# Two chained attention and feed-forward layers: operands loaded by chunk, position rows made once, four small moves between engines

## The chip, the cores and the metric

The kernel runs on one core of a Trainium2 chip. The metric is the device time in microseconds (us) of one execution; lower is better. The core has a matmul engine (TensorE, PE), VectorE (DVE), ScalarE (ACT), GpSimd (POOL) and SyncE (SP), which issues DMAs here; each runs its own list of instructions in order and waits on semaphores for the others.

## The reference

All matrices have 256 columns, x has 2048 rows. Cut to what matters:

```python
xn = layernorm(x)
s  = linear_attention(xn)              # cumulative sums over the rows, 16 heads of 16
g  = silu(xn @ ternary(weight).T + b)
x  = x + s * g                         # layer 0
xn = layernorm(x)
q, k, v = split(xn @ qkv_w.T + qkv_b)  # 16 heads of 16 columns
scores = q @ k.T / 4 + slope[h] * (pos_k - pos_q), causal
s  = softmax(scores) @ v @ out_w.T + out_b
# 8 experts, the top 2 of each row:
y_e = (glu * sigmoid(1.702 * glu) * (lin + 1)) @ w2[e].T + b2[e]
g  = silu(sum over the two chosen e of weight_e * y_e)
x  = x + s * g                         # layer 1
```

## The kernel before

**Layer 0** runs over four chunks of 512 rows (`NC` = 4, `CH` = 512). In each engine's list `front(c)` has the projections and cumulative sums of a chunk and `back(c)` the quotient, the gate and the sum into x. On ACT the order is `front(c + 1)`, `high_parts(c)` (first halves of two experts' first weights), `back(c)` (L685 to L694). On DVE it is `front(c + 1)`, `back(c)`, `gate(c)` (L985 to L995), and `gate(c)` reads what ACT's `back(c)` writes. On POOL it is `front(c + 1)`, `low_parts(c)` (second halves of those weights, which count up `w1l_done`), `back(c)`. SP issues 23 DMAs at L339 that fill the buffer of routed rows `x_rows` with zeros, and then, in a loop over chunks, waits for `w1l_done`, fetches the next two experts' raw weights (L326) and stores x (L351).

**Projection of layer 1** (L712 to L731, L1027 to L1041, L1327 to L1348) makes q and k of a chunk as three bf16 parts each, in `QP`, which is part of the operand tile `OPS`. SP stores them in the DRAM tensor `parts` (L357). When all four chunks are stored, `load(h)` (L360) reads the operands of a head back into `OPS` with six DMAs, three for each side; each takes one, two or three parts, or one part several times over (`LOADS`, L35), 48, 32 or 16 partitions of 4 KB. Four head slots exist, so `load` runs for two heads (a pair) at a time, and the next pair but one is loaded when the scores of a pair are done (L423 to L427). Twelve more operand rows carry position times slope: ACT makes them for heads 0 to 3 (`first_of`, L763), POOL for the others (`rows`, L524).

**Main loop** (`for n in range(STEPS)` in the lists of all engines, 684 steps). A pair of heads has 80 tiles (`PER_PAIR`), there are 8 pairs, 640 tiles. Step n has

- `score_a(n)` on PE and `reduce_a(n)` on DVE: scores of 128 rows against up to 512 keys, only for the row maxima. The tile lies in one of four banks for n < 44 (`WIDE`), then in one of two, so `score_a(n)` waits for `reduce_a(n - 2)` (L1422).
- `score_b(n - 44)` on PE and `exponential(n - 44)` on ACT (`LEAD` = 44): the same scores transposed, less the row maxima, in two banks; `values` multiplies them with v, four tiles at a time.
- At the end of a chunk of A tiles: `row_maxima` (DVE), `maxima` (POOL, L536), `turn_maxima` (PE, at the steps `TURN_AT`), `max_rows` (ACT) and `rows_out` (SP, two DMAs at L377), which puts the maxima into the operands that B tiles of this chunk use 44 steps later. `ORDER` is the order of a pair's chunks; chunk a has 8 (a + 1) tiles.
- Every 20 steps one block of 256 routed rows: `fetch_block` on SP (five DMAs, L403 to L407), `up` and `down` on PE, `gate_tanh`, `gate_linear`, `expert_out` on ACT, `glu`, `linear` on DVE, `store_block` on SP. There are 23 blocks; block b starts at step 84 + 20 b, is fetched at step 66 + 20 b or earlier, as SP's list allows. `down` and `turn_maxima` and the heads' outputs share bank 7.

Between projection and main loop the routing is worked out: ranks of the logits and one-hot rows (DVE, L1079 to L1110), first parts of x (ACT, L773) and second parts (POOL, L560), 32 indirect DMAs that scatter the rows (POOL, `scatter`, L565), and the experts' output biases, by weights turned on PE, matmuls and copies on ACT (L776 to L784). In the last pair POOL gathers the experts' results (`gather`, L573), two indirect DMAs for each of 16 row tiles, 12 of them before `maxima(28)` (L600), and DVE sums them (`add_experts`, L1065). The end of the kernel projects and gates the output.

Of the kernel before, what the change touches and what calls it, by code (L numbers as in the profile page):

```python
# [14 lines left out]
ALU = mybir.AluOpType  # L15
# [3 lines left out]
P = 128  # L19
# [17 lines left out]
ROWS_B = ROWS_A + 3  # L37

ORDER = (0, 3, 1, 2)
# [12 lines left out]
FIRST_BLOCK, EVERY = 84, 20  # L52
# [30 lines left out]
TURN_AT = {chunk_end(m) - 1 + (3, 4, 5, 3)[m % NC]: m for m in range(NC * PAIRS)}  # L83
HEADS_AT = {chunk_end(m) - 1 + LEAD + (15, 11, 11, 11)[m % NC]: m for m in range(NC * PAIRS)}
BLOCK_AT = {FIRST_BLOCK + EVERY * b: b for b in range(BLOCKS)}
DOWN_AT = {n + 14: b for n, b in BLOCK_AT.items()}
FETCH_AT = {n - 18: b for n, b in BLOCK_AT.items()}
STORE_AT = {n + 1: b for n, b in DOWN_AT.items()}
STEPS = TOTAL + LEAD
END_PAIRS = [2 * c + r for c in ORDER for r in range(2)]  # L90
END_AT = {650: 0, 655: 1, 661: 2, 665: 3, 675: 4, 679: 5}
ADD_AT = {FIRST_BLOCK + EVERY * BLOCKS + 28 + 3 * n: t
          for n, t in enumerate([2 * q + r for q in END_PAIRS for r in range(2)])}
GATHERS = 6
# [8 lines left out]
def build(nc, x, w_qkv0, w_out0, w_ffn, b_ffn, w_qkv1, b_qk1, b_v1, w_out1, b_out1, slopes, pos_rows, pick,  # L103
          masks, ident, sel, table, gate_w, gate_b, w1, b1, w2, b2, out):
    ctx = ExitStack()
    with ctx:
# [3 lines left out]
        def sem(name):  # L110
# [39 lines left out]
        TH = sb("TH", [P, 2, CH])  # L150
        GT = sb("GT", [P, 2, CH])
# [9 lines left out]
        WE = sb("WE", [P, NT, E])  # L161
# [22 lines left out]
        XTH, XTL = XT[:, 0], XT[:, 1]  # L184
        WQG = 3 * D + E
# [9 lines left out]
        WET = pr32[:, 0:S]  # L195
        B2 = pr32[:, S:S + D]
        TAB = pr32[:, S + D:S + D + E * NT + 8 + 24]
# [7 lines left out]
        YB = xt32[:, 0:1024].rearrange("p (b n) -> p b n", b=2)  # L205
        GB = xt32[:, 1024:1024 + 512 * GATHERS].rearrange("p (g a d) -> p g a d", g=GATHERS, a=2)
# [18 lines left out]
        QV = ops32[:, 0:2048].rearrange("p (m n) -> p m n", m=4)  # L225
        QR = ops32[:, 2048:4096].rearrange("p (m n) -> p m n", m=4)
        QP = ops32[:, 4096:7168].bitcast(BF16).rearrange("p (m j n) -> p m j n", m=4, j=3)


        parts = nc.dram_tensor("qk_parts", (2, 3, D, S), BF16, kind="Internal").ap()  # L230
        x_rows = nc.dram_tensor("x_rows", (SLOTS * BLOCKS, 2 * D), F16, kind="Internal").ap()
# [29 lines left out]
        v_copied, lg_copied, gsplit, route = (  # L261
            sem("v_copied"), sem("lg_copied"), sem("gsplit"), sem("route"))
        expd, rstep, ones_rows, we_done, wet_ps = (
            sem("expd"), sem("rstep"), sem("ones_rows"), sem("we_done"), sem("wet_ps"))
        wet_copied, b2_ps, acc_init, b1_prep, slope_part = (
            sem("wet_copied"), sem("b2_ps"), sem("acc_init"), sem("b1_prep"), sem("slope_part"))
        scl, opa_rows, vs_ready, a_scored, a_reduced = (
            sem("scl"), sem("opa_rows"), sem("vs_ready"), sem("a_scored"), sem("a_reduced"))
# [8 lines left out]
        hot, count_ps, chain, slots_done, xr_high, xr_low = (  # L277
            sem("hot"), sem("count_ps"), sem("chain"), sem("slots_done"), sem("xr_high"), sem("xr_low"))
# [10 lines left out]
        b2_zero, wet_zero = sem("b2_zero"), sem("wet_zero")  # L289
# [3 lines left out]
        ones_in, first_rows = sem("ones_in"), sem("first_rows")  # L293
# [27 lines left out]
        def _(sp):  # L321
# [1302 lines left out]
```

## Time and profile before

| | us |
|---|---|
| median of 3 runs (970.33 to 974.29) | 972.36 |
| profiled execution, its own time | 969.48 |
| its span | 967.7 |

Busy time over the span and idle time before the costliest groups, of the page of the profile:

```profile
span 967.7 us, 13783 instructions
...
PE 796.4 (82%) x4910; PEld 387.1 (40%) x4910; DVE 635.3 (66%) x1197; ACT 498.7 (52%) x1030; POOL 313.9 (32%) x363
...
PE   4474659914889999999999999999999995888986
PEld 1242345403324444444544444444444432222543
DVE  5999997665856666676566667666666763984121
ACT  2343315861555565555555655555565552556340
POOL 2766963121660060051006005100600516340111
PEclk9797979966799999999999999999999997999795
DMA  9501302332223235225223532522353112111110
```

Each digit is the busy share of one of 40 slices of 24.2 us, in tenths; PEclk is the clock granted to TensorE, DMA the mean share of the 16 DMA engines. The first eight slices are layer 0 and the projection, slices 9 and 10 are a hole in PE's row, then comes the main loop, with PE at nine tenths, and the last six slices are the last pair of heads and the output.

### The profile page before, as it was taken

Reading aid. Unit: us, or ns where it says so; the run is one execution under the profiler, and the core shown is the slowest. Engines: PE = TensorE matmul, PEld = TensorE weight load, DVE = VectorE, ACT = ScalarE, POOL = GpSimd, SP = SyncE. Lnnn points to the kernel's source line nnn. Section 1 sums busy time; section 2 is a strip of 40 time slices with the busy share of each in tenths; the row PEclk is TensorE's granted clock in tenths of the full one; section 3 lists DMA queues with packets and bytes.
Section 4 is the critical chain, followed back from the end, with each engine's and each line's share of the span. In section 5 each row is a group of like instructions: output and inputs, shape, how many; then the busy total and the mean of one; then the engine's idle time right before and its main releaser. Section 6 shows DMA issues by size and latency. Waiting matters only on the chain.

```text
span 967.7 us, 13783 instructions
## 1 busy us (share of the span) xinstructions
PE 796.4 (82%) x4910; PEld 387.1 (40%) x4910; DVE 635.3 (66%) x1197; ACT 498.7 (52%) x1030; POOL 313.9 (32%) x363
## 2 busy tenths in 40 slices
PE   4474659914889999999999999999999995888986
PEld 1242345403324444444544444444444432222543
DVE  5999997665856666676566667666666763984121
ACT  2343315861555565555555655555565552556340
POOL 2766963121660060051006005100600516340111
PEclk9797979966799999999999999999999997999795
DMA  9501302332223235225223532522353112111110
GB/s 322 173 0 66 109 22 87 131 108 70 102 93 88 67 99 100 76 63 107 62 66 103 101 73 65 106 62 66 98 108 71 40 49 77 45 55 68 42 34 33
DMA packets 72392, 80.03 MB, mean 83 GB/s; under 512 B 33561, under 2 KB 56020, under 8 KB 72196
## 3 DMA queue, kind: packets, MB, share of 16 engines
q1 hardware_dynamic: 67660, 68.84, 26.0%
q0 software_dynamic: 3296, 8.62, 2.9%
q10 hardware_dynamic: 1368, 1.70, 0.6%
q8 instruction: 39, 0.64, 0.3%
q14 instruction: 29, 0.24, 0.1%
HBM read 34.22 MB, written 26.74 MB: 63 GB/s over the span
## 4 chain that ended last, share of the span: by engine, by line
PE 55%; DVE 26%; issue 7%; POOL 3%; DMA 3%; ACT 3%; SPq 1%; POOLq 0%; ACTq 0%; DVEq 0%
PE bank L1466 14%; DVE PM L1163 11%; PE bank L1424 10%; PE bank L1444 7%; PE bank L1361 5%; PE bank L1371 5%; PE bank L1481 3%; DVE PR L960 3%; PE bank L1256 2%; PE bank L1508 2%; DMA OPS<-qk_parts 2%; DVE YT L1062 2%; POOL XT L580 1%; POOL x_rows L569 1%; PE bank L1427 1%
## 5 line engine op out<-in xcount | busy, mean ns | idle before, releaser
L1163 DVE TENSOR_REDUCE PM<-bank 128x1 f32<-128x512 f32 (+3 forms) x640 | 368.6, 605 | 217.7 <-PE bank L1427 160.1
L811 ACT ACTIVATE PR<-bank 128x512 f32<-128x512 f32 (+3 forms) x640 | 331.6, 536 | 302.7 <-PE bank L1447 150.7
L1424 PE MATMUL bank<-OPS 108*128 108x512 bf16 (+3 forms) x640 | 228.5, 361 | 72.3 <-DVE PM L1163 36.1
L1444 PE MATMUL bank<-OPS 111*128 111x512 bf16 (+3 forms) x640 | 225.0, 354 | 3.3 <-ACT PR L811 3.1
L1466 PE MATMUL bank<-PR,VS 128*17 128x512 f32 (+3 forms) x1280 | 159.0, 548 | 0.5 <-ACT PR L811 0.4
L540 POOL TENSOR_TENSOR NP<-NM,NIL 128x8 bf16<-128x8 f32 x32 | 6.5, 202 | 429.9 <-DVE NM L1171 429.8
L1424 PEld LDWEIGHTS bank<-OPS 108*128 108x128 bf16 x640 | 64.2, 100 | 193.3 <-DVE PM L1163 131.9
L1361 PE MATMUL bank<-WB 128*128 128x256 f16 x552 | 90.7, 272 | 0.0
L527 POOL TENSOR_TENSOR OPS<-POSR,SCL 12x2048 bf16<-12x2048 bf16 x24 | 87.8, 3680 | 7.6 <-PE bank L1447 7.6
L1444 PEld LDWEIGHTS bank<-OPS 111*128 111x128 bf16 x640 | 63.3, 99 | 39.0 <-ACT PR L811 15.6
L1361 PEld LDWEIGHTS bank<-WB 128*128 128x128 f16 x552 | 49.5, 99 | 44.6 <-issue 22.3
L1427 PE MATMUL bank<-MASK 128*128 128x128 bf16 x256 | 57.7, 225 | 0.0
L1447 PE MATMUL bank<-MASK 128*128 128x128 bf16 x256 | 57.4, 225 | 0.0
L1299 PE MATMUL bank<-VV,YT 128*128 128x256 f32 x64 | 21.4, 506 | 36.1 <-DVE YT L964 36.1
L1256 PE MATMUL bank<-XT,VV 128*128 128x512 f16 x144 | 35.2, 407 | 13.1 <-issue 11.6
L1371 PE MATMUL bank<-WB,YT 128*128 128x256 f32 x184 | 45.9, 392 | 0.0
L1481 PEld LDWEIGHTS bank<-SEL,U 128*128 128x128 f32 x256 | 32.1, 197 | 26.3 <-issue 26.3
L1371 PEld LDWEIGHTS bank<-WB,YT 128*128 128x128 f32 x184 | 33.1, 189 | 23.1 <-issue 19.5
L1466 PEld LDWEIGHTS bank<-PR,VS 128*17 128x17 f32 x1280 | 21.3, 96 | 49.2 <-issue 29.0
L580 POOL DMA_INDIRECT XT<-y_rows,SLOT x32 | 30.9, 966 | 18.2 <-DVE ACC L1075 9.8
L1481 PE MATMUL bank<-SEL,U 128*128 128x34 f32 x256 | 35.7, 286 | 0.8 <-ACT U L800 0.8
L569 POOL DMA_INDIRECT x_rows<-XT,SLOT x32 | 31.0, 968 | 14.1 <-issue 9.1
(187 smaller groups left out, 975.8 us busy)
## 6 DMA issues: line engine op xcount, KB each, us to landing
qk_parts<-OPS SPq DMA_DIRECT2D x16, 384.0 KB, 3.6
OPS<-qk_parts SPq DMA_DIRECT2D x32, 192.0 KB
x_rows<-PR SPq DMA_DIRECT2D x23, 256.0 KB, 3.6
WB<-W1H SPq DMA_DIRECT2D x23, 256.0 KB, 2.4
WB<-W1L SPq DMA_DIRECT2D x23, 256.0 KB, 2.4
WB<-in_w SPq DMA_DIRECT2D x23, 256.0 KB, 2.7
y_rows<-XT SPq DMA_DIRECT2D x23, 256.0 KB, 2.2
OPS<-qk_parts SPq DMA_DIRECT2D x32, 128.0 KB
```

The source lines that it names most:

```text
L527: pool.tensor_tensor(OPS[0:POS, h % 4, side, :], POSR[:, side, :], SCL[:, side, h:h + 1].broadcast_to([POS, S]), ALU.mult).then_inc(opa_ro ...
L811: act.activation(PR[:, tile % RING, off:CH], PS[2 + tile % 2][:, off:CH], ACT.Exp).then_inc(b_exped, 1)
L1163: dve.tensor_reduce(PM[:, c % 2, j, xq, gg:gg + 1], bank[:, 0:width], AX.X, ALU.max).then_inc(a_reduced, 1)
L1256: done = mm(out, w if weight_first else d, d if weight_first else w, start=first and k == 0 and j == 0, stop=last and k == KK - 1 and j == 2)
L1361: last = mm(PS[5 + f][:, SLOTS * part:SLOTS * part + SLOTS], W1B[b % 2][:, wp, col:col + P], XB[b % 2][:, dp, k, :], start=j == 0, stop=j ...
L1371: last = mm(PS[7][:, D * q:D * q + D], YT[:, b % 2, f, P * q:P * q + P], W2B[b % 2][:, f, :], start=f == 0, stop=f == KK - 1)
L1424: last = mm(bank[:, 0:width], OPS[0:ROWS_A, h % 4, 0, P * (TC * a + xq):P * (TC * a + xq) + P], OPS[0:ROWS_A, h % 4, 1, CH * gg:CH * gg + ...
L1427: last = mm(bank[:, P * xq:P * xq + P], MASK[:, 0, :], MASK[:, 2, :], start=False, stop=True)
L1444: last = mm(bank[:, off:CH], OPS[0:ROWS_B, h % 4, 1, P * k:P * k + P], OPS[0:ROWS_B, h % 4, 0, CH * b + off:CH * b + CH], start=True, stop ...
L1447: last = mm(bank[:, off:off + P], MASK[:, 1, :], MASK[:, 2, :], start=False, stop=True)
L1466: last = mm(PS[4][32 * n:32 * n + HD + 1, off:CH], VS[:, (2 * p + j) % 4, k, :], PR[:, (first + n) % RING, off:CH], start=b > 0 and k0 == ...
L1481: last = mm(PS[7][:, wide * q:wide * q + wide], U[:, m % 2, P * q:P * q + P], SEL[:, :], start=True, stop=True)
```

## The change

- `load(h)` stays for heads 2 and up. Heads 0 and 1 are loaded by chunk of 512 rows (`first_load(c)`, 14 DMAs each), issued by SP between the stores of the parts. For that `QV`, `QR`, `QP` move out of `OPS`. `score_a` waits for the chunk alone that it needs.
- The position rows of all heads are made once: POSR has 96 partitions (8 heads of 12), ACT makes four tiles of 96x2048 in layer 0 (`position_rows`), SP stores them in DRAM, and each `load` has a seventh DMA that reads them. The slopes' parts (`prepare`, DVE) move into layer 0.
- The 23 DMAs of zeros move behind the first wait for `w1l_done` on SP.
- `rows_out` moves from SP to ACT, one step after `max_rows`.
- The output bias of an expert is fetched with its block (`B2B`) and added by DVE as it empties the block's bank (`expert_out` moves from ACT to DVE); the turned weights, their matmuls and copies go.
- A tiles use three banks from tile 44 on; both halves of a block's first product use one bank, the second half nine steps behind the first. `fetch_block` waits for `ye_copied`, the copy of the block two before, instead of `ye_ps`, and has six DMAs.
- `ORDER` becomes (0, 1, 2, 3); blocks start at step 88 + 20 b, are fetched at 72 + 20 b; scatters and gathers are dealt out otherwise between the `maxima`.
- Ranks are worked out by chunk (5 operations each), the rest of the sort is 28 small operations, two in a step of the main loop.

```diff
             sp.dma_start(TAB[:, :], table).then_inc(table_in, 16)
-            sp.wait_ge(memset_done, 11)
-            for r in range(0, SLOTS * BLOCKS // P, 2):
-                sp.dma_start(x_rows[P * r:P * r + 2 * P, :].rearrange("(r p) c -> p r c", p=P),
-                             NAUGHT[:, :].unsqueeze(1).broadcast_to([P, 2, 2 * D])).then_inc(rows_zero, 16)
-
             for c in range(NC):
                 if c + 2 < E // 2:
                     sp.wait_ge(w1l_done, 2 * c + 2)
                     fetch_experts(c + 1)
+                if c == 0:
+                    sp.wait_ge(memset_done, 11)
+                    for r in range(0, SLOTS * BLOCKS // P, 2):
+                        sp.dma_start(x_rows[P * r:P * r + 2 * P, :].rearrange("(r p) c -> p r c", p=P),
+                                     NAUGHT[:, :].unsqueeze(1).broadcast_to([P, 2, 2 * D])).then_inc(rows_zero, 16)
+                    for n in range(4):
+                        sp.wait_ge(rows_made, n + 1)
+                        sp.dma_start(all_rows[n // 2, :, n % 2, :], PROWS[n % 2]).then_inc(rows_kept[n % 2], 16)
...
+            def first_load(c):
+
+                cols = slice(CH * c, CH * c + CH)
+                sp.wait_ge(parts_out[0], 16 * c + 16)
+                sp.wait_ge(parts_out[2], 16 * c + 16)
+                for h in range(2):
+                    sp.dma_start(OPS[0:POS, h, :, cols], all_rows[0, POS * h:POS * h + POS, :, cols]).then_inc(first_in[c], 16)
+                    for side in range(2):
...
+            for c in range(NC):
+                cols = slice(CH * c, CH * c + CH)
+                for m in range(4):
...
+                    sp.wait_ge(qk_p2, 4 * c + m + 1)
+                    sp.dma_start(parts[side, :, half * P:half * P + P, cols].rearrange("j f t -> f j t"),
+                                 QP[m]).then_inc(parts_out[m], 16)
+                if c:
+                    first_load(c - 1)
+            first_load(NC - 1)
...
                 if b >= 2:
-                    sp.wait_ge(ye_ps, b - 1)
+                    sp.wait_ge(ye_copied, b - 1)
...
             for n in range(STEPS):
-                if n - 1 in TURN_AT:
-                    rows_out(TURN_AT[n - 1])
                 if n in FETCH_AT:
                     fetch_block(FETCH_AT[n])
...
-            scatter(range(0, 5))
+            scatter(range(0, 4))
             maxima(1)
-            scatter(range(5, 11))
+            scatter(range(4, 12))
             maxima(2)
-            scatter(range(11, NT))
+            scatter(range(12, NT))
             maxima(3)
...
-                    gather(0, GATHERS)
+                    gather(0, 3)
                 maxima(NC * p)
                 if p == PAIRS - 1:
-                    gather(GATHERS, 11)
+                    gather(3, 8)
...
+            def position_rows():
+
+                act.wait_ge(scl, 6)
+                act.wait_ge(cast_in, 32)
+                for n in range(4):
+                    if n >= 2:
+                        act.wait_ge(rows_kept[n % 2], 16)
+                    act.activation(PROWS[n % 2], POSR[:, n % 2, :], ACT.Copy, scale=SCL[:, n % 2, n // 2:n // 2 + 1])\
+                        .then_inc(rows_made, 1)
...
                 high_parts(c)
+                if c == 0:
+                    position_rows()
                 back(c)
...
                 if tile < WIDE:
                     wait(pe, a_reduced, tile - 3)
                 else:
-                    pe.wait_ge(a_reduced, tile - 1)
-                bank = PS[tile % 4] if tile < WIDE else PS[tile % 2]
+                    pe.wait_ge(a_reduced, tile - 2)
+                if tile == WIDE:
+                    pe.wait_ge(sorting, SORTED)
+                bank = PS[tile % 4] if tile < WIDE else PS[(0, 1, 6)[tile % 3]]
```

## Rows read from the trace of the kernel before

**Rows 1.** Busy time by stretch: from:to, length, engines, TensorE's clock, DMA share, GB/s
```profile
198.00:230.00 32.00, 0.08 (x2) 0.06 (x2) 15.11 (x46) 12.47 (x17) 10.51 (x12) 0.54 0.33 110
...
313.60:398.10 84.50, 78.96 (x552) 38.91 (x550) 55.37 (x108) 49.29 (x108) 19.25 (x26) 1.00 0.35 82
...
796.30:884.00 87.70, 69.20 (x419) 23.92 (x416) 60.55 (x124) 42.60 (x88) 35.33 (x52) 0.88 0.17 49
```
**Rows 2.** Waits of PE from 313.6 to 778 us: total, times, longest
```profile
PE bank L1424 <- DVE PM L1163: 24.8, 56, 1.0
```
**Rows 3.** Timeline, layer 0: start, length, engine, line, operation
```profile
54.89 0.59 ACT L671 ACTIVATE TH<-bank 128x512 f32<-128x512 f32 x1
...
60.54 2.36 DVE L970 SCALAR_TENSOR_TENSOR GT<-TH,GT 128x512 f32<-128x512 f32 x2
...
60.80 1.55 POOL L476 TENSOR_TENSOR PR<-OPS 128x512 f32<-128x512 f32 x1 [7.30 <-DVE YT L964]
...
73.36 2.14 POOL L505 TENSOR_TENSOR W1L<-W1L,W1H 128x1024 f16<-128x1024 f32 x1
...
75.52 0.36 SPq L326 DMA_DIRECT2D W1H<-in_w  x1
```
**Rows 4.** Timeline, SP's zeros, and busy time while they are moved
```profile
15.27 18.43 SPq L339 DMA_DIRECT2D x_rows<-PR  x23
...
20.00:32.00 12.00, 7.38 (x40) 3.74 (x37) 11.72 (x36) 6.19 (x13) 7.99 (x6) 1.00 1.08 379
```
**Rows 5.** Groups by form, ACT, 198 to 260 us: count, then busy, mean ns
```profile
L766 ACT ACTIVATE OPS<-POSR,SCL 12x2048 bf16<-12x2048 bf16 x8 | 15.3, 1987 | 4.7 <-DMA qk_parts<-OPS 4.7
```
**Rows 6.** Timeline, DVE: part of `prepare`; one form alone, then beside POOL
```profile
160.67 0.77 DVE L1020 SCALAR_TENSOR_TENSOR SCL<-SLP,PICK,SCL 12x16 f32<-12x16 bf16 x4
...
207.26 0.28 DVE L1097 TENSOR_TENSOR U<-U,LG 128x128 f32<-128x128 f32 x1
...
217.15 1.19 DVE L1107 TENSOR_TENSOR U<-U,TOP 128x128 f32<-128x128 f32 x1
```
**Rows 7.** Timeline and busy time, loads of heads 0 to 3 and PE's first score
```profile
203.20 12.05 SPq L369 DMA_DIRECT2D OPS<-qk_parts  x12
...
229.97 0.27 PE L1424 MATMUL bank<-OPS 108*128 108x128 bf16 x1 [31.92 <-DMA OPS<-qk_parts]
...
203.00:230.00 27.00, 0.03 (x1) 0.06 (x2) 10.65 (x28) 11.94 (x13) 10.51 (x12) 0.50 0.22 72
```
**Rows 8.** First pair: the line of the B scores; timeline of reductions, scatters, step 80
```profile
L1444 PE MATMUL bank<-OPS x640: 219/379/634, 259.0 to 941.5; 111*128 111x512 bf16 x128, 111*128 111x256 bf16 x32
...
244.36 12.30 DVE L1163 TENSOR_REDUCE PM<-bank 128x1 f32<-128x512 f32 x22
...
244.41 0.99 POOL L569 DMA_INDIRECT x_rows<-XT,SLOT  x1 [0.30 <-issue]
...
293.08 0.22 PE L1424 MATMUL bank<-OPS 108*128 108x128 bf16 x1
```
**Rows 9.** Timeline, SP in the main loop, then one landing of L407
```profile
430.98 11.99 SPq L369 DMA_DIRECT2D OPS<-qk_parts  x12
...
452.28 5.43 SPq L407 DMA_TRANSPOSE WB<-x_rows  x1
...
DMA to landing us min/median/max: 9.3/9.3/9.3
```
**Rows 10.** Timeline, last pair: gathers and PE's wait, and clock behind it
```profile
799.07 1.04 POOL L580 DMA_INDIRECT XT<-y_rows,SLOT  x1 [0.56 <-issue]
...
815.47 0.27 PE L1474 MATMUL bank<-MASK,NP 128*24 128x128 bf16 x1 [10.23 <-POOL NP L548]
...
815.50:822.00 6.50, 6.50 (x27) 2.62 (x27) 3.06 (x6) 2.43 (x5) 1.93 (x2) 0.52 0.13 33
```
**Rows 11.** Prices: issue on SP; DVE from a bank, by form
```profile
L377 SPq DMA_DIRECT2D OPS<-MT x64: 698/762/2429, 255.8 to 888.7; - x64
...
L978 DVE SCALAR_TENSOR_TENSOR GT<-bank,GT 128x512 f32<-128x512 f32 x8 | 5.3, 680 | 0.6 <-PE bank L1299 0.6
```

More of the change, by code:

```diff
@@ L351, in _ @@
                 sp.dma_start(x1_dram[:, TC * c:TC * c + TC, :], XO[:, TC * c:TC * c + TC, :]).then_inc(x1_spill, 16)
-            with sp.Fori(0, NC) as c:
-                for m in range(4):
-                    side, half = m // 2, m % 2
-                    sp.wait_ge(qk_p2, 4 * c + m + 1)
-                    sp.dma_start(parts[side, :, half * P:half * P + P, ds(c * CH, CH)].rearrange("j f t -> f j t"),
-                                 QP[:, m, :, :]).then_inc(parts_out[m], 16)
             def load(h):
+                sp.dma_start(OPS[0:POS, h % 4, :, :], all_rows[h // 8, POS * (h % 8):POS * (h % 8) + POS, :, :]).then_inc(
+                    opa_in[h // 2 % 2], 16)
                 for side in range(2):
@@ L387, in _ @@
                              ONEB[0:3, :].unsqueeze(1).broadcast_to([3, NC, CH])).then_inc(ones_in, 16)
+            for m in range(4):
+                sp.wait_ge(parts_out[m], 16 * NC)
             load(2)
@@ L517, in _ @@
             rstd(2 * NC, ds(TC * (NC - 1), TC))
-            pool.wait_ge(outT, 2 * NC)
-            pool.memset(WET[:, :], 0.0).then_inc(wet_zero, 1)
-            scale(E // 2 - 1)
-            pool.wait_ge(w1l_done, E - 2)
-            low_parts(E // 2 - 1)
-            def rows(h):
-                for side in range(2):
-                    pool.tensor_tensor(OPS[0:POS, h % 4, side, :], POSR[:, side, :],
-                                       SCL[:, side, h:h + 1].broadcast_to([POS, S]), ALU.mult).then_inc(opa_rows, 1)
             def head_values(h):
@@ L1021, in prepare @@
                                                  ALU.mult, ALU.add).then_inc(scl, 1)
[L1023 to L1025 removed]
+            front(0, True)
+            for c in range(NC):
+                if c + 1 < NC:
+                    front(c + 1, c + 2 < NC)
+                if c == NC - 1:
+                    gated(c - 1)
+                    norm_apply(0, NC)
+                back(c)
+                gate(c)
+                if c:
+                    next_stats(c - 1)
@@ new lines, in rank @@
+            def rank(c, k):
+                tiles = slice(TC * c, TC * c + TC)
+                own = LG[:, tiles, :].unsqueeze(3).broadcast_to([P, TC, E, E])
+                other = LG[:, tiles, :].unsqueeze(2).broadcast_to([P, TC, E, E])
+                lower = TAB[:, E * NT + 32:].rearrange("p (e f) -> p e f", e=E).unsqueeze(1).broadcast_to([P, TC, E, E])
+                if c == 0 and k == 0:
+                    dve.wait_ge(table_in, 16)
+                if k == 0:
+                    dve.wait_ge(lg_copied, TC * c + TC)
+                wait(dve, ranked, 5 * c + k)
+                if k == 0:
+                    ins = dve.tensor_tensor(RIVAL, other, own, ALU.is_gt)
+                elif k == 1:
+                    ins = dve.tensor_tensor(EQUAL, other, own, ALU.is_equal)
+                elif k == 2:
+                    ins = dve.tensor_tensor(EQUAL, EQUAL, lower, ALU.mult)
+                elif k == 3:
+                    ins = dve.tensor_tensor(RIVAL, RIVAL, EQUAL, ALU.add)
+                else:
+                    ins = dve.tensor_reduce(RANK[:, tiles, :], RIVAL, AX.X, ALU.add)
+                ins.then_inc(ranked, 1)
@@ L1069, in add_experts @@
                 dve.wait_ge(y_gathered[place % GATHERS], 32 * (place // GATHERS + 1))
-                if place == 0:
-                    dve.wait_ge(acc_init, NT // 2)
-                for a in range(2):
-                    if a:
-                        dve.wait_ge(half_added, place + 1)
-                    dve.scalar_tensor_tensor(
-                        ACC[:, t, :], GB[:, place % GATHERS, a, :], WTS[:, a, t:t + 1],
-                        ACC[:, t, :], ALU.mult, ALU.add).then_inc(y_added if a else half_added, 1)
@@ L1157, in reduce_a @@
+                ins.then_inc(sorting, 1)
             def reduce_a(tile):
```

436 lines of the change are left out of this document (198 added, 238 removed).

## The prediction

> **What bounds the kernel now.** I read the busy times by stretch first. There is a hole: from 198 to 230 us TensorE is all but idle, and a pair of the main loop takes 84.50 us with TensorE busy 78.96 [rows 1]. So the main loop is TensorE's, the hole is somebody else's. The timeline names it: the first score ends a wait of 31.92 us for the operands [rows 7]. Next the waits of PE in the loop: 24.8 us in 5.5 pairs, 4.5 us a pair, for reductions of DVE [rows 2]; there is no other wait of size. Last the lists of ACT, POOL and SP wherever the change moves something, since a moved DMA takes its place in a queue with it. In layer 0 DVE works without a break, so a microsecond lost there is lost at the end.
>
> Times below are against the profiled execution: 969.48, of which 967.7 is the span; the median of the runs, 972.36, is 2.9 above it, and I add that at the end.
>
> **1. Layer 0: position rows and zeros.** ACT's new `position_rows` stands between `high_parts(0)` and `back(0)`. Its third tile reuses the first one's buffer and waits until SP's store of the first has landed. On SP that store now stands behind the wait for `w1l_done` of 2, the fetch of two experts and the 23 zeros. Before, `w1l_done` reached 2 at 75.5 (73.36 + 2.14), and SP's fetch starts then [rows 3]. ACT's `back(0)` began at 54.89 and DVE's gate, which needs it, at 60.54 [rows 3]. So the wait that is added queues ACT's gate of chunk 0 behind it, and DVE behind that. In order:
> - DVE first runs `prepare`, 11 operations, four of which took 0.77 [rows 6]: 2.1 us. It then releases POOL at 62.9 instead of 60.8; with DVE idle POOL's six products and two differences run undisturbed. I take 74.7 for `w1l_done` (bounds 73 and 77.6).
> - The experts are 1 MB, 2.8 us at the 379 GB/s of the zeros' stretch [rows 4], say 3.5 with their start: 79 us. The zeros took 18.43 us to issue, paced by the queue, 6.0 MB at that rate being 15.9 us [rows 4]: I take 16.5, so 95.5. The store behind them needs some 2.5 us to land: 98. Then two tiles of 1.92 us (15.3 for 8) [rows 5]: 102. ACT's tanh and copy give the first gate 1.1 later, 103.
> - DVE starts its gate at 103 instead of 60.5: 42.5 us. It gets some back, since POOL has finished what disturbed it: a form that takes 0.28 alone took 1.19 beside POOL [rows 6]. I take 4.5 off.
>
> Sum: **+38** (bounds 33 and 44). The earlier place of the zeros hid them beside DVE's work; the new one has no cover, as ACT, DVE and PE all wait for it. The larger POSR load (eight times the rows) is among the first DMAs, which fill the engines: +1.
>
> **2. The hole.** Operands of chunk 0 are issued after the stores of chunk 1, near 176, 14 DMAs; 12 took 12.05 us [rows 7], 1 us each, though the first came faster, so 10 to 14 us a chunk against chunks that come every 11 to 12 us. `first_load(0)` lands before 190; the score of tile 0 can start when projection ends, at 198.5, 31.5 us earlier. The later chunks (needed at tiles 8, 24 and 48) keep ahead. What is late next is DVE: from 198.5 it must do two rankings (10 operations), 28 operations of sorting, and the first 44 reductions. 22 reductions took 12.30 us, 0.56 each [rows 8]: 24.6; 38 operations at 0.3, 11.4; and POOL's second parts of x now run beside them, +3. So tile 44 comes at 198.5 + 39 = 237.5, where the first B score was at 259.0 [rows 8]: 21.5 us are left. Next POOL: a scatter is issued every 1.26 us (0.99 and a pause of 0.30) [rows 8]. The second group is now 16 scatters, 20.2 us, after `maxima(1)` near 229; `maxima(2)` follows at 251 while PE wants it at step 52, near 243.5. A wait of 7, where there were two of 1.2 and 2.6 before: 4 us back. Step 80, at 293.1 before [rows 8], comes at 276: **-17** (bounds -8 and -25).
>
> **3. The main loop's waits.** With the third bank `score_a(n)` waits for the reduction of n - 3, one step (1.05 us) more slack than the longest wait of 1.0 [rows 2] needs: -4.5 a pair. DVE's new work, four bank emptyings a pair at 0.68 [rows 11], brings it from 55.4 to 58.1 of 82 us [rows 1]; it hides. ACT loses four copies and gains eight DMA issues a pair at 0.76 on SP [rows 11], two in a row 1.5 us; its B tiles have two banks, so about 1 us of slack: +0 to +1 each time, and +0.5 for `expert_out` ahead of a turn. A DMA issue on ACT between B tiles does not occur before; I take the price of SP's. Net -2.2 a pair, 6 pairs: **-13** (bounds -26 and +12).
>
> **4. Block fetches behind operand loads.** This is the edit I weigh most after the first. A pair's load is 2 heads of 768 KB. In the hole it ran at 72 GB/s with the DMA engines 0.22 busy [rows 7]: its copies of 48 and 32 partitions keep few engines busy, and what comes after on SP's queue waits for those. In the loop: load issued at 430.98, the block fetch that follows it has its last DMA issued at 452.28 and landed 9.3 later, 461.6: 30.6 us after the load began [rows 9]. Before, that fetch was for the block of step 84, 38 steps after the load's place at step 46, and nothing waited. Now count modulo 80: the load goes out when step 44 begins, as SP is free; a fetch stands at step 52 behind it and its block starts at step 68. 24 steps of 1.03 us are 24.7, plus 0.7 in the step. The fetch is whole at 31.4 (30.6 and the seventh DMA of each head): TensorE waits 6. It loses clock too: after the 10.23 us wait the clock was at 0.52, half of 2.4 GHz, for 6.5 us [rows 10]; for a wait of 6 I take 1.5 us. Five loads (pairs 1 to 5) have such a fetch, the sixth has none: 5 x 7.5 = **+38** (bounds 0, if the fetch overtakes the load, and +55).
>
> By the Trainium skill (DMA: Bandwidth & Descriptors, "Why a DMA increments its semaphore by 16 and not by 1") a copy runs on the largest number of engines up to 16 that divides both outer sizes, and on the lowest-numbered ones; that gives 3, 2 and 16 engines for the three shapes, so engine 0 carries a third, a half and a sixteenth of them. At that page's 27 GiB/s an engine (Specifications) the load would be an estimated 18 us, the fetch would be whole before step 68, and part 4 would be near 0. The row of 27 us says otherwise.
>
> **5. The last pair.** 12 gathers stood before `maxima(28)`, from 799.07, and TensorE waited 10.23 us [rows 10]. Now there are 6, 7.6 us after step 559, over before the turn at step 572. The wait goes, and with it half the 6.5 us at half clock; the third bank gives another 1: **-14** (bounds -5 and -20). Late next is DVE, 60.6 busy of 87.7 [rows 1]. GATHERS of 5 leaves 15 steps from gather to sum: enough.
>
> The rest (order of chunks, one bank for a block's halves, biases) I cost at +1, for the stores that queue behind `first_load`. A pair's 80 tiles are the same in any order.
>
> **Sum:** +38 +1 -17 -13 +38 -14 +1 = +34: 1003.5 for the profiled execution, 1006 for the median.
>
> **Rivals.**
> - A: block fetches don't wait. For it: block weights are copies on all engines, a small part on the busy ones. Against it: the 30.6 us of [rows 9]. 1006 - 38 = 968. The Trainium skill's figures, weighed in part 4, would give this case too.
> - B: layer 0 hides the position rows. It would need SP's store to land before 60 us, which the wait for `w1l_done` at 75.5 forbids [rows 3], or the zeros not to hold it up. The latter alone leaves 22 of 38. 1006 - 38 = 968, or with A as well 930.
> - C, on the slow side: ACT's DMA issues. Each of some 28 row maxima sent in the loop keeps ACT for 2 x 0.76 [rows 11]. Once ACT lags by more than the step that two B banks allow, all of that delay is TensorE's: 1.4 us each instead of the 0.5 counted above, 28 x 0.9 = 25 more, 1031.
> - D: the change does what it says and its gains stand alone, 930 to 940; that is A and B together.
>
> **How the numbers follow.** My forecast 0.64, A 0.17, B 0.07, A with B 0.04, C 0.08. Range 962 to 1032: it takes in A and B at 968, and the bounds of parts 1 and 4 above; their own range in the likeliest case is 985 to 1030. About 0.5% (5 us) is what a measurement here can tell from no change. Faster by more (below 967.5): half of A and B and all of A with B, 0.16. Within: the other half, 0.10. Slower: 0.74.
>
> **What would show it.** Part 1: ACT idle from about 59 to 98 us, its `back(0)` near 101, DVE idle over the same time and SP's 23 zeros starting near 76. Part 2: the first score at 198.5 plus the delay of part 1, PE waiting for `maxima(2)`. Part 3: no wait of `score_a` for DVE in the loop, small waits of `score_b` for ACT. Part 4: five waits of `up` for `block_in`, 6 us each, 80 steps apart, each with a fall of the clock. Part 5: no wait of 10 us at `maxima(28)`. I am wrong if DVE's gate of chunk 0 starts before 80 us, or if `up` never waits.

## The result and the profile after

The changed kernel takes 992.51 us in the median of 4 runs (990.12 to 996.16), the kernel before 971.35 beside it (969.40 to 974.29): a ratio of 1.0219, 95% interval 1.0176 to 1.0261. It is slower by 21 us. The profiled execution took 991.7, its span is 989.8. The forecast was 1006, with 962 to 1032 as range and 0.74 on slower.

The page of the changed kernel; each digit is a slice of 24.7 us:

```profile
span 989.8 us, 13708 instructions
...
PE   4520775795679997997899799969988999889996
DVE  6940799888857674675466466646664666797121
ACT  2330621584046653664455366535644555556541
PEclk9765887897579998999899899979998999999995
DMA  8009111144333046227223623362263231250000
```

Slices 3 and 4 of DVE (4, 0) and PE (2, 0) are a new hole in layer 0, where DVE stood at 9 before; the old hole, a 1 and a 4 in PE's slices 9 and 10, is now a 5 and a 6 in slices 10 and 11; and in the main loop PE drops to 8, 7 or 6 every few slices, and PEclk to 8 or 7 with it, where it had an unbroken row of nines. To see what each was worth I read the same milestones in every trace: the starts of `score_a` of tiles 0, 80 and 560 and of the last one, and the end. Here they are for the two kernels and the experiments on chips alike ("pairs" is tile 80 to tile 560, six pairs; "end" tile 560 to the end):

| kernel | median us | ratio, 95% | tile 0 | tile 80 | pairs | end |
|---|---|---|---|---|---|---|
| before | 971.35 | 1 | 230.0 | 293.1 | 503.1 | 171.5 |
| changed | 992.51 | 1.0219, 1.0176 to 1.0261 | 233.0 | 309.9 | 531.3 | 148.6 |
| e4_whole | 1022.26 | 1.0557, 1.0502 to 1.0611 | 265.4 | 336.5 | 529.9 | 152.7 |
| e5_two_banks | 1009.54 | 1.0407, 1.0351 to 1.0463 | 233.4 | 311.4 | 545.3 | 153.2 |
| e6_rows_sp | 1008.88 | 1.0402, 1.0348 to 1.0457 | 233.0 | 321.4 | 534.7 | 150.0 |
| e12_rows_again | 962.40 | 0.9915, 0.9891 to 0.9939 | 201.4 | 278.4 | 531.1 | 148.7 |
| e9_both | 916.77 | 0.9443, 0.9409 to 0.9476 | 205.0 | 280.9 | 481.4 | 152.6 |
| e10_both_two_banks | 943.57 | 0.9728, 0.9681 to 0.9775 | 204.1 | 281.2 | 508.4 | 151.3 |
| e11_both_rows_sp | 909.46 | 0.9374, 0.9328 to 0.9420 | 204.8 | 282.2 | 475.3 | 150.3 |
| e8_before_spread | 957.72 | 0.9880, 0.9829 to 0.9931 | 216.1 | 282.8 | 504.8 | 167.1 |

By it the change cost 16.8 up to tile 80, cost 28.2 in the six pairs, and gave 22.9 back at the end: 22.1 of span in all.

**Layer 0**, the timeline of the changed kernel: start, length, engine, line, in brackets the wait before it and who ended it. The first two lines are ACT's `position_rows`, then ACT's gate, DVE's gate, and SP's list.

```profile
55.49 3.88 ACT L683 ACTIVATE WB<-POSR,SCL 96x2048 bf16<-96x2048 bf16 x2
97.94 3.89 ACT L683 ACTIVATE WB<-POSR,SCL 96x2048 bf16<-96x2048 bf16 x2 [38.56 <-DMA position_rows<-WB]
101.74 0.57 ACT L673 ACTIVATE TG<-bank 128x512 f32<-128x512 f32 x1
...
102.83 0.69 DVE L966 SCALAR_TENSOR_TENSOR TG<-TG 128x512 f32<-128x512 f32 x1 [41.03 <-ACT TG L674]
...
74.46 0.35 SPq L332 DMA_DIRECT2D W1H<-in_w  x1
74.85 0.43 SPq L332 DMA_DIRECT2D W1L<-in_w  x1
75.32 18.04 SPq L350 DMA_DIRECT2D x_rows<-PR  x23
93.41 8.75 SPq L354 DMA_DIRECT2D position_rows<-WB  x4
...
148.39 37.87 SPq L360 DMA_DIRECT2D x_rows<-XO  x3
```

Read from below: SP could not store a position row before its fetch at 74.46 and the zeros, 18.04 long. The first store goes out at 93.41 and ACT goes on at 97.94; so ACT stood 38.56 and DVE 41.03. The last store of x ends at 186.26 (148.39 + 37.87); in the kernel before it ended at 150.71:

```profile
112.91 37.80 SPq L351 DMA_DIRECT2D x_rows<-XO  x3
```

**The main loop**, waits of PE in it (total, times, longest), and the first of the long ones with the fetch that ended it; L1381 is `up`, L1423 `score_a`, L1443 `score_b`:

```profile
PE bank L1381 <- DMA WB<-x_rows: 38.5, 5, 9.3
PE bank L1443 <- ACT PR L806: 7.0, 6, 1.2
PE bank L1423 <- DVE PM L1181: 1.8, 5, 0.4
...
351.65 0.37 SPq L364 DMA_DIRECT2D OPS<-position_rows  x1
...
371.16 6.88 SPq L431 DMA_TRANSPOSE WB<-x_rows  x1
...
DMA to landing us min/median/max: 3.4/7.2/11.1
...
382.28 0.82 PE L1381 MATMUL bank<-WB 128*128 128x256 f16 x3 [6.49 <-DMA WB<-x_rows]
```

The load goes out at 351.65, the last DMA of the fetch behind it at 371.16 and lands 11.1 later (the largest of the two in that window), at 382.3: 30.6 us after the load began, as in [rows 9]. PE's waits for DVE that stood in [rows 2] are gone but for 1.8 us.

### The profile page after: what moved, and what is told of

Same layout as the page of the kernel before. It is cut to its first block, busy times and chain, and to the rows that moved or that the text cites. A ratio compares the mean times of both kernels' runs of the same rounds, so it can differ in the third digit from the quotient of the medians.

```text
span 989.8 us, 13708 instructions
## 1 busy us (share of the span) xinstructions
PE 793.1 (80%) x4861; PEld 379.6 (38%) x4862; DVE 623.2 (63%) x1208; ACT 474.6 (48%) x991; POOL 227.9 (23%) x337
## 4 chain that ended last, share of the span: by engine, by line
PE 45%; DVE 15%; SPq 11%; POOL 8%; DMA 8%; issue 8%; ACT 4%; ACTq 1%; POOLq 0%; DVEq 0%
PE bank L1465 10%; PE bank L1443 9%; PE bank L1423 7%; SPq L373 6%; DMA WB<-x_rows 6%; PE bank L1381 5%; PE bank L1391 4%; POOL XT L587 3%; DVE PR L956 3%; POOL x_rows L576 2%; PE bank L1480 2%; SPq L350 2%; PE bank L1322 2%; PE bank L1506 2%; ACT PR L806 2%
## 5 line engine op out<-in xcount | busy, mean ns | idle before, releaser
L1181 DVE TENSOR_REDUCE PM<-bank 128x1 f32<-128x512 f32 (+3 forms) x640 | 364.4, 604 | 228.2 <-PE bank L1426 127.8
L806 ACT ACTIVATE PR<-bank 128x512 f32<-128x512 f32 (+3 forms) x640 | 327.3, 534 | 324.6 <-PE bank L1443 203.2
L1423 PE MATMUL bank<-OPS 108*128 108x512 bf16 (+3 forms) x640 | 234.1, 371 | 16.3 <-DVE PM L1181 15.2
L1443 PE MATMUL bank<-OPS 111*128 111x512 bf16 (+3 forms) x640 | 227.4, 358 | 13.1 <-ACT PR L806 11.1
L1381 PE MATMUL bank<-WB 128*128 128x256 f16 x552 | 94.1, 280 | 38.5 <-DMA WB<-x_rows 38.5
L1423 PEld LDWEIGHTS bank<-OPS 108*128 108x128 bf16 x640 | 66.1, 103 | 111.1 <-DVE PM L1181 87.0
L1443 PEld LDWEIGHTS bank<-OPS 111*128 111x128 bf16 x640 | 63.2, 99 | 89.0 <-ACT PR L806 65.9
L1381 PEld LDWEIGHTS bank<-WB 128*128 128x128 f16 x552 | 49.4, 100 | 77.3 <-DMA WB<-x_rows 40.7
L1279 PE MATMUL bank<-XT,VV 128*128 128x512 f16 x144 | 37.3, 425 | 12.9 <-DVE XT L868 12.4
L1322 PEld LDWEIGHTS bank<-VV,YT 128*128 128x128 f32 x64 | 17.1, 275 | 74.9 <-ACT TG L674 52.6
L1480 PEld LDWEIGHTS bank<-SEL,U 128*128 128x128 f32 x256 | 31.0, 191 | 26.2 <-issue 21.7
L966 DVE SCALAR_TENSOR_TENSOR TG<-TG 128x512 f32<-128x512 f32 x8 | 7.4, 954 | 41.3 <-ACT TG L674 41.3
```

What stands on the lines that cost most here:

```text
L806: act.activation(PR[:, tile % RING, off:CH], PS[2 + tile % 2][:, off:CH], ACT.Exp).then_inc(b_exped, 1)
L1181: dve.tensor_reduce(PM[:, c % 2, j, xq, gg:gg + 1], bank[:, 0:width], AX.X, ALU.max).then_inc(a_reduced, 1)
L1322: last = mm(PS[6 + r][:, D * q:D * q + D], OT0[:, k, P * (2 * r + q):P * (2 * r + q) + P], WO0[:, k, :], start=k == 0, stop=k == KK - 1)
L1381: last = mm(PS[5][:, SLOTS * part:SLOTS * part + SLOTS], W1B[b % 2][:, wp, col:col + P], XB[b % 2][:, dp, k, :], start=j == 0, stop=j == 5)
L1423: last = mm(bank[:, 0:width], OPS[0:ROWS_A, h % 4, 0, P * (TC * a + xq):P * (TC * a + xq) + P], OPS[0:ROWS_A, h % 4, 1, CH * gg:CH * gg + ...
L1443: last = mm(bank[:, off:CH], OPS[0:ROWS_B, h % 4, 1, P * k:P * k + P], OPS[0:ROWS_B, h % 4, 0, CH * b + off:CH * b + CH], start=True, stop ...
```

## The experiments

Four kernels (e1, e2, e3, e7) fell on a chip on which every kernel is longer: the kernel before took 992.43 there (987.07 to 996.03), against 970 to 971 elsewhere. The traces say in part how. Waits of PE in e3_spread, 200 to 340 us:

```profile
PE bank L1441 <- issue: 6.9, 3, 2.9
PE bank L1441 <- ACT PR L804: 6.8, 3, 3.3
PE bank L1421 <- issue: 4.0, 8, 1.6
```

"issue" means that the engine waited for nothing the profile shows. In e9_both, elsewhere, the same code and stretch has 0.6 us of it. These pauses sit in the first pair and the last, hardly in the loop. Times there scatter more too, and the traces of e1 and e7 are of their shortest executions (990.45 and 1002.15). So of these four I read ratios to the kernel before on the same chip, and from the traces layer 0 and the loop.

**One part of the wait in layer 0.** The zeros go back to their old place, the stores of position rows stay behind the wait for `w1l_done`.

```diff
             sp.dma_start(TAB[:, :], table).then_inc(table_in, 16)
+            sp.wait_ge(memset_done, 11)
+            for r in range(0, SLOTS * BLOCKS // P, 2):
+                sp.dma_start(x_rows[P * r:P * r + 2 * P, :].rearrange("(r p) c -> p r c", p=P),
...
             for c in range(NC):
...
                 if c == 0:
-                    sp.wait_ge(memset_done, 11)
-                    for r in range(0, SLOTS * BLOCKS // P, 2):
...
```

> The changed kernel with the 23 DMAs of zeros back in their old place, ahead of the wait for w1l_done; the four stores of the position rows stay behind that wait. It splits the wait: theory says the stores start at 75 us instead of 93.4 and land near 80, so 17 to 18 us of ACT's 38.6 us wait go and 20 stay; 974 to 977 us. If the zeros were no part of it, nothing changes and it is 992; if they were all of it, 957.

Measured: 1000.16, ratio 1.0089 (1.0052 to 1.0127); against 1.0219 that is 1.3%, 12.6 us, where 15 to 18 were expected. In the trace the last store of x ends at 170.51, 15.75 earlier than in the changed kernel, and tile 0 starts at 217.0, 16.0 earlier:

```profile
131.26 39.25 SPq L360 DMA_DIRECT2D x_rows<-XO  x3
```

So the zeros are 16 us of the wait, and the rest is the wait for `w1l_done`.

**The whole of it.** The stores ahead of both.

```diff
             sp.dma_start(TAB[:, :], table).then_inc(table_in, 16)
+            for n in range(4):
+                sp.wait_ge(rows_made, n + 1)
+                sp.dma_start(all_rows[n // 2, :, n % 2, :], PROWS[n % 2]).then_inc(rows_kept[n % 2], 16)
             for c in range(NC):
...
-                    for n in range(4):
-                        sp.wait_ge(rows_made, n + 1)
...
```

> The changed kernel with one block of SP's list moved: the four stores of the position rows stand ahead of the wait for w1l_done, the fetch of two experts and the 23 zeros; all else as in the changed kernel. Theory (the order of SP's list makes the 41.0 us wait of DVE for ACT's first gate): the first store lands near 62 us, ACT's back(0) starts near 67 instead of 101.7, DVE waits some 5 us instead of 41, and the kernel is 30 to 36 us faster than the changed one, 957 to 962. Rival (the loss in layer 0 comes from the four tiles of 96x2048 and the larger load themselves): ACT is still late by more than 20 us and the kernel gains under 15.

> The changed kernel with the four stores of position rows ahead of the wait for w1l_done, once more, on another chip, since all engines of the chip of the first look stood still for 1 to 3 us at many places that no wait explains. From the kernel with both remedies (step 80 at 280.9 against 309.9) and the ratio of the first look (986.3 to 992.4) the edit is worth 27 to 30: 962 to 966.

Measured: 986.26 on the first chip, with four runs from 974.66 to 994.27, too far apart for a ratio; on another chip 962.40, ratio 0.9915 (0.9891 to 0.9939). Against the changed kernel's 992.5 that is 30 us, as expected, and tile 80 comes 31.5 earlier. Timeline of SP and DVE in e12:

```profile
62.09 2.19 SPq L345 DMA_DIRECT2D position_rows<-WB  x2
76.18 18.29 SPq L353 DMA_DIRECT2D x_rows<-PR  x23
117.12 37.80 SPq L360 DMA_DIRECT2D x_rows<-XO  x3
...
64.95 3.35 DVE L966 SCALAR_TENSOR_TENSOR TG<-TG 128x512 f32<-128x512 f32 x2 [3.22 <-ACT TG L674]
```

DVE's gate starts at 64.95 instead of 102.83, and of the 35.5 us that the last store of x had lost, 31.3 are back. With this one reordering the change is 0.9% faster than the kernel before.

**The block fetch behind the load.** The load's copies of 48 and 32 partitions become copies of 16.

```diff
                     for first, parts_of, times_of in LOADS[side]:
-                        src = parts[side, first:first + parts_of, HD * h:HD * h + HD, :]
-                        if times_of > 1:
-                            src = src.broadcast_to([times_of, HD, S])
-                        sp.dma_start(OPS[row:row + rows, h % 4, side, :], src).then_inc(opa_in[h // 2 % 2], 16)
+                        for part in list(range(first, first + parts_of)) * times_of:
+                            sp.dma_start(OPS[row:row + HD, h % 4, side, :],
+                                         parts[side, part, HD * h:HD * h + HD, :]).then_inc(opa_in[h // 2 % 2], 16)
+                            row += HD
```

> The changed kernel with each operand load for heads 2 and up cut into copies of 16 partitions (twelve for a head instead of six, the same bytes; first_load as it was). Theory (the copies of 48 and 32 partitions run on 3 and 2 DMA engines, so a pair's 1.5 MB take 27 us): the copies of 16 partitions run on 16 engines, the load takes as long as its 26 issues, 16 to 18 us, the DMA share while it runs rises, the fetch behind it is whole near step 65 of 68, and the waits of up for block weights fall from 38.5 to under 8 us: 957 to 968 us. Rival (the load is bound by its bytes or by DRAM): waits and time stay.

Measured: 971.33, ratio 0.9810 (0.9748 to 0.9872), 4.1% or 40 us below the changed kernel, where 25 to 35 were expected. The six pairs take 481.4 instead of 531.3, 49.9 less, and no wait of `up` for a DMA is left. Both remedies together:

> The changed kernel with two mends at once: the position rows' stores ahead of the wait on SP, and operand loads of heads 2 and up in copies of 16 partitions. If the two losses of the changed kernel are these and are independent, the gains add: 30 to 36 and 25 to 34 us, 925 to 937 us, some 4% under the kernel before the change.

Measured: 916.77, ratio 0.9443 (0.9409 to 0.9476); six pairs again 481.4, tile 80 29.0 earlier than in the changed kernel. Both kernels are beaten, by 5.6% the one before, and the 925 to 937 expected too. Against e12, which lacks the spread alone, the spread is worth 45.6 us; by the traces 49.7 in the six pairs, less 2.5 up to tile 80 and 3.9 behind tile 560, and no run resolves why those two are longer. What the edit did to the load is seen in the busy times of stretches: in the changed kernel load issued, fetch issued, fetch landing, in e9 load issued, then fetch issued and landed (the last two columns are the DMA share and GB/s).

```profile
351.60:363.90 12.30, 11.97 (x92) 6.83 (x90) 8.81 (x18) 6.38 (x16) 1.68 (x7) 1.00 0.26 83
363.90:371.00 7.10, 7.07 (x50) 3.09 (x48) 5.44 (x11) 5.44 (x11) 0.00 (x0) 1.00 0.54 162
371.00:382.30 11.30, 4.46 (x35) 2.10 (x35) 4.41 (x10) 2.32 (x7) 0.00 (x0) 0.88 1.14 96
```

```profile
322.60:335.80 13.20, 12.84 (x94) 7.04 (x93) 9.68 (x21) 7.20 (x18) 1.69 (x7) 1.00 0.49 127
335.80:343.20 7.40, 7.40 (x56) 3.87 (x55) 4.70 (x9) 4.64 (x10) 0.00 (x0) 1.00 0.73 212
```

While SP issues, the share of busy DMA engines is 0.49 instead of 0.26, at 127 instead of 83 GB/s. Length times GB/s, summed, is some 3.3 MB in either kernel, moved in 30.7 and in 20.6 us. By the landings in the traces, a load in the loop is whole 26.9 to 28.8 us after its start in the changed kernel and 14.8 to 15.8 in e9. The last DMA of the fetch goes out at 339.71 and lands 3.5 later:

```profile
339.71 1.32 SPq L429 DMA_TRANSPOSE WB<-x_rows  x1
...
DMA to landing us min/median/max: 3.5/3.5/3.5
```

343.2 is 20.6 us after the load began at 322.63, 10.0 less than in the changed kernel and inside the 24.7 that the steps give. By the Trainium skill (DMA: Bandwidth & Descriptors, "Why a DMA increments its semaphore by 16 and not by 1") copies whose outer size is 16 use 16 engines where those of 48 and 32 partitions, by their parts, use 3 and 2. By that rule the trace agrees: same bytes, twice the share.

**The other order.** Loads go six steps later, behind the fetch.

```diff
-                p, rest = divmod(n - LEAD - 2, PER_PAIR)
+                p, rest = divmod(n - LEAD - 8, PER_PAIR)
```

> The changed kernel with the operand loads six steps later in SP's list, so that the block fetch of step 52 goes ahead of them. Theory (this fetch waits behind the load's bytes on the few DMA engines that it keeps busy): the five waits of TensorE for block weights, 38.5 us in all, go; but the load now ends near step 81 of its pair, just after the next pair needs it, so that 1 to 6 us a pair come back as a wait of score_a for operands or of the next block. 965 to 985 us. Rival (block fetches are slow for another reason, such as ACT's DMAs or the six DMAs of a fetch): the waits of up stay near 38 us and the time stays at 992 or rises.

Measured: 1012.93, ratio 1.0226 (1.0173 to 1.0278), no gain. Waits of PE in its loop:

```profile
PE bank L1423 <- DMA OPS<-qk_parts: 28.0, 5, 6.1
```

The expectation failed because the load has no slack either: six steps later, the first score of the next pair but one waits for it, 28.0 us in 5 times instead of 38.5. The six pairs are 10.7 shorter in its trace (520.6), yet the median doesn't show it; how much of that chip's pauses fell on this kernel I can't tell apart, so the size stays open. The cause is settled all the same: the slow load is what is late, in either order; in the loop here it is whole 26.5 to 28.4 us after its start.

**Loading by chunk.** Heads 0 and 1 loaded whole after the last store.

```diff
-                if c:
-                    first_load(c - 1)
-            first_load(NC - 1)
+            for m in range(4):
+                sp.wait_ge(parts_out[m], 16 * NC)
+            first_load(0)
...
-                cols = slice(CH * c, CH * c + CH)
+                cols = slice(0, S)
```

> The changed kernel with heads 0 and 1 loaded whole after all stores (14 DMAs of 2048 columns), as before the change, instead of by chunk. Theory: the first score waits some 28 to 31 us for operands, but DVE has its last ranking behind it by then and POOL its second parts, so the 44 first tiles take about 34 instead of 39 us, and PE's waits for maxima(2) change little: 20 to 27 us slower than the changed kernel, 1012 to 1020. Rival (DVE or POOL set the end of this stretch anyway, the head start is given back whole): under 8 us slower.

Measured: 1022.26, ratio 1.0557 (1.0502 to 1.0611), 29.8 above the changed kernel; 20 to 27 were expected. The first score waits as it did in [rows 7]:

```profile
265.42 0.26 PE L1421 MATMUL bank<-OPS 108*128 108x128 bf16 x1 [33.07 <-DMA OPS<-qk_parts]
```

Tile 0 is 32.4 later, tile 80 26.6: during the wait DVE does 3.3 us of its work and POOL 11.0, and the first 44 tiles take 32.9 instead of 39.2, so 5.8 of it is hidden. Behind tile 560 4.1 more are lost, whose cause stays open.

**Load spread in the kernel before**, the same edit as e3 alone:

> The kernel before with one edit: its operand loads in copies of 16 partitions each (24 DMAs where there were 12). Nothing in its main loop waited for a load, so its pairs stay at 84.5. The load in the hole, 31.9 us of waiting, should shrink to the issue of 24 DMAs of SyncE and their landing, some 16 to 22 us. Theory: 956 to 964. Rival: the hole is bounded by what runs beside the load (scatters, VectorE's sort), as in the changed kernel where TensorE waited for VectorE until tile 44: 966 to 972.

Measured: 957.72, ratio 0.9880 (0.9829 to 0.9931), inside the 956 to 964 of the theory.

```profile
216.14 0.26 PE L1422 MATMUL bank<-OPS 108*128 108x128 bf16 x1 [18.36 <-DMA OPS<-qk_parts]
```

The hole's wait goes from 31.92 [rows 7] to 18.36 and tile 0 comes 13.8 earlier. Its inner pairs stay at 84.5, so spreading the load does nothing for a loop in which nothing waits for it.

**The third bank.**

```diff
-                    pe.wait_ge(a_reduced, tile - 2)
+                    pe.wait_ge(a_reduced, tile - 1)
-                bank = PS[tile % 4] if tile < WIDE else PS[(0, 1, 6)[tile % 3]]
+                bank = PS[tile % 4] if tile < WIDE else PS[tile % 2]
```

> The changed kernel with the A tiles back in two banks from tile 44 on, so that score_a(n) waits for the reduction of n - 2. Theory: its waits for DVE, 1.8 us over six pairs, come back at 4 to 5 us a pair; outside the stretches where PE waits for block weights anyway: 20 to 30 us slower, 1012 to 1022. Rival (the kernel is held by ACT or by the block weights, and the third bank only moves waits): under 8 us slower.

> The kernel with both remedies (position rows stored ahead, operand loads in copies of 16 partitions; 916.8) with its third bank of A scores given back: score_a(n) waits for the reduction of n - 2 again. In the changed kernel itself the bank was worth 17 us in all, but there the pairs held other waits that it may have shared. Theory: the bank alone carries the shorter pair. 80.9 becomes 84 to 85 (TensorE waits for VectorE again, 4 to 4.5 us a pair in more than 40 small waits), and the whole is 19 to 26 slower: 936 to 943. Rival: the bank matters only beside the disturbances of the block fetches, and the other edits (fewer copies on ScalarE, larger emptyings) carry the pair: 918 to 926.

Measured: in the changed kernel 1009.54, 17.0 more, under the 20 expected, since the bank's waits take from those for fetches (26.7 in its loop, where 38.5 stood); in the kernel with both remedies 943.57 against 916.77, 26.8 more, just past the 19 to 26 expected, and the inner pairs go from 80.9 to 85.3. Waits of PE in its loop:

```profile
PE bank L1421 <- DVE PM L1179: 19.6, 47, 1.0
PE bank L1441 <- ACT PR L804: 5.4, 6, 0.9
```

The bank is worth 4.4 us a pair. The rival, that other edits carry the shorter pair, falls: without the bank the pair is 0.8 longer than the 84.5 before.

**Who issues the row maxima.** Back to SP.

```diff
-                act.wait_ge(mt_copied, m + 1)
+                sp.wait_ge(mt_copied, m + 1)
                 for j in range(2):
-                    act.dma_start(OPS[ROWS_A:ROWS_B, (2 * p + j) % 4, 0, CH * a:CH * a + CH].rearrange(
+                    sp.dma_start(OPS[ROWS_A:ROWS_B, (2 * p + j) % 4, 0, CH * a:CH * a + CH].rearrange(
...
-                if n - 2 in TURN_AT:
-                    rows_out(TURN_AT[n - 2])
+                if n - 1 in TURN_AT:
+                    rows_out(TURN_AT[n - 1])
```

> The changed kernel with rows_out back on SP. Theory: ACT loses 64 issues of some 0.7 us, its B tiles wait less (score_b waited 7.0 us for ACT over six pairs) and SP issues each pair of row DMAs ahead of the operand load or behind it; between 6 us faster and 4 slower, 986 to 996. Rival 1 (ACT's issues cost TensorE 1 us each and more): 20 us faster or more. Rival 2 (row maxima behind an operand load on SP's queue come too late for the B tiles): over 8 us slower, with waits of score_b for DMA.

> The same kernel with the DMAs of the row maxima issued by SyncE, where the kernel before had them, instead of ScalarE. In the changed kernel this made 16 us, and the trace named waits of score_b of 8.8 us for rows behind the operand loads. Theory: the price is the order on SyncE's queue, behind 26 copies a pair and behind the second half of the first load. The loads are more DMAs now but land sooner, so the waits shrink to 2 to 6 us a pair: 928 to 945. Rival: nothing but the length of the load in flight counted, and with short loads the issuing engine makes no difference: 914 to 920.

Measured: in the changed kernel 1008.88, 16.4 more. The theory's 986 to 996 is missed; it is rival 2, over 8 us slower by waits of `score_b` for rows that come too late. Waits of PE in its first pair and in its loop:

```profile
PE bank L1443 <- DMA OPS<-MT: 18.8, 1, 18.8
...
PE bank L1443 <- DMA OPS<-MT: 42.4, 5, 8.8
```

The rows of the first two chunks were ready at 249.8 and 265.1. SP issued their four DMAs at 274.9 to 277.7, right behind the loads of heads 2 and 3. They landed at 291.4 and 291.7, 14 to 17 us after their issue, and PE waited until 291.66. In the changed kernel ACT issued them at 249.80 and 265.13, the latter in the midst of the same loads. They landed at 253.3 and 271.8, 3.5 and 6.7 later, and no `score_b` waited for them, the first of which started at 272.97. So a short DMA queued on SP right behind a slow load landed late, and one on ACT's queue passed it. By the Trainium skill (DMA: Bandwidth & Descriptors, "Queues, rings and completion order") SP and ACT each have their own ring on every DMA engine, and an engine takes turns between the rings it has work for. By that rule the trace agrees.

Most of the 16.4 is this one place: tile 80 comes 11.5 later. In the loop it is SP's list alone: the rows that ACT issues at 362.5 in the changed kernel go out on SP at 389.50, behind the load and the fetch, and land 5.1 later, at 394.6, with PE waiting for 8.73. These waits, 42.4 in all, stand where the 38.5 for fetches stood, and the six pairs are only 3.5 longer.

With the loads spread, the same edit has the other sign: 909.46 against 916.77, inner pairs 79.9 instead of 80.9, and the waits for ACT are all but gone. PE in the loop of e9, then of e11:

```profile
PE bank L1441 <- ACT PR L804: 7.4, 8, 1.2
```

```profile
PE bank L1441 <- ACT PR L806: 0.4, 2, 0.2
```

Both the theory (928 to 945) and the rival (914 to 920) were off: neither had counted what ACT gets back, 1.0 a pair and 2.9 behind the last score. e11 is the fastest kernel of this study, 6.3% below the one before.

## Why the prediction was right, and where its sizes were off

Direction and mechanisms held; the sum of +34 was +22.1 of span (989.8 - 967.7). By its parts:

- **Part 1, layer 0: right.** DVE's gate was forecast at 103 and came at 102.83; SP's fetch at 74.7, and 74.46; the zeros 16.5 long, and 18.04. That 103 was hit so closely is luck: the fetch held the zeros up by 0.9 and not 4.3 (they began at 75.32 and not at 79), the zeros took 1.5 more, and the store 4.5 to land (93.41 to 97.94) and not 2.5. The 38 is 35.5 by the last store of x (186.26 against 150.7 before). e1 puts 16 of it on the zeros, as rival B had it (38 less 22), and e12 gives 31.3 of 35.5 back. The +1 for the POSR load has no row of its own and is in the 35.5.
- **Part 2, the hole: right.** With the delay of 35.5 the first score was due at 234.0 and came at 233.0; the 39 us for 44 tiles were 39.2, the wait of 7 for `maxima(2)` was 6.0, and -17 was -18.7 (16.8 less 35.5). What bounds this stretch is DVE, as forecast: PE waits 17 times for its reductions there, 12.0 us.
- **Part 3, the loop: right, small by 9.** Free of fetch waits the six pairs are 481.4 against 503.1, -21.7 where -13 stood. The bank's -4.5 a pair was 4.4. The term that was mis-sized is ACT's: I counted +2.3 a pair, e11 says 1.0. The issue itself was priced well (0.72 us for each, two in a row 1.47), but only 1.2 of it reaches PE at most, and not at every turn.
- **Part 4, fetches behind loads: right, small by 12.** Five waits, 80 steps apart. But +38 was +49.9. The waits are 7.7 each and not 6: TensorE reaches the block 24.1 us after the load begins and not 25.4, its steps being shorter than I took, and the fetch is whole 30.6, 31.9, 31.0, 33.4 and 32.1 after it, 31.8 in the mean, where 31.4 stood. Why that differs from pair to pair no run resolves. And what they cost beyond is 2.3 each, not 1.5. The granted clock of the changed kernel, while PE waits and after:

```profile
376.00:382.20 6.20, 0.00 (x0) 0.00 (x0) 0.52 (x1) 0.42 (x1) 0.00 (x0) 0.80 0.31 96
382.30:390.50 8.20, 8.20 (x40) 4.30 (x40) 2.93 (x6) 2.36 (x5) 0.00 (x0) 0.74 0.01 2
```

  PE is busy for the whole 8.2 us at 0.74 of 2.4 GHz: a fall to 1.2 GHz for part of it, which costs 2.1 us (8.2 x 0.26). e9, without these waits, has 1.00 over the whole loop.
- **Part 5, the last pair: right, small by 9.** The 10 us wait at `maxima(28)` is gone; 3.9 in two waits is left. -14 was -22.9, past my bound of -20. Two sizes were off: the clock over the whole pair, 0.98 instead of 0.88, with which as many matmuls took 63.61 instead of 69.40 busy, 5.8 where I had 3.2; and the 5.1 us by which the tail behind the last score is shorter (78.5 against 83.6), for which I had no term at all. PE is busy 4.7 less in it (64.18 against 68.85), with 306 matmul records against 321 and a clock of 0.85 against 0.80. The last pair of 70.1, the same in e12, is also a short one: e9 has 72.8, e4, e5, e6, e10 and e11 73.1 to 73.4. Why, no run resolves.

```profile
841.20:911.30 70.10, 63.61 (x420) 23.30 (x419) 57.47 (x124) 41.79 (x88) 35.68 (x52) 0.98 0.29 91
```

Parts 3 and 5 took 18 more off and part 4 put 12 more on, parts 1, 2 and the rest 6 less: 34 becomes 22. That these errors cancel in part is luck. The chances add up to 0.12 within and 0.72 slower, not 0.10 and 0.74. Rival A fell with the five waits, B with DVE's gate at 102.83, D with both. Rival C, ACT's issues, is real in kind and a third of its price: 7.0 us of waits in the loop, 7.3 us in all by e11. What it left out is the other side of the same move, which e6 shows: with the loads as slow as they are, SP's queue would have cost 16.4 more.

## What to carry to other kernels

A store that frees a buffer should not stand behind a wait it has no part in: one such place on a queue held three engines for 38 us, and moving three lines gave back 30. Look at how many DMA engines a transfer keeps busy, not at its bytes: a slow load does no harm until something is queued behind it, and then each edit that shares its queue is priced by it. And price an edit again after its neighbours change: the row maxima on ScalarE were worth 16 us beside the slow loads, most of it in the first pair, and cost 7 beside fast ones.

## What the runs showed of the hardware

- The same load was whole 26.9 to 28.8 us after its start in copies of 48, 32 and 16 partitions, and 14.8 to 15.8 in copies of 16 alone. In the trace of the kernel before, a load's 12 copies tell their semaphore 92 times, in e8 its 24 copies 384 times, 16 each: the four copies of 16 make 64 of the 92, and the eight wider ones 28.
- Copies of 16 partitions cost SP hardly more to issue than half as many larger ones: 24 took 12.2 us (5.53 and 6.68), 12 took 11.3 (3.89 and 7.41).
- A short DMA on ACT's queue passed the loads in flight on SP's (landed 6.7 us after its issue, 2.5 where nothing was in flight), one on SP's queue did not (14 to 17 us).
- One chip was 2.2% slower than the others for the same kernel (992.43 against 971), by pauses, most of 1 to 3 us, that no semaphore explains and most of which lie in the first and last pair. PE has 19.4 to 22.0 us of them behind 200 us in each of the four traces there, and at most 0.6 in any other. The profile puts further waits of DVE and ACT there down to "remote", a name that no other trace has. Why there, no run here shows.
